# Weighting the attention logits and taking their maximum in one VectorE operation instead of two

## The reference, cut to what matters

```python
h = jnp.einsum('ni,hio->hno', x, W)                 # 4 heads, 64 features each
attn_src = jnp.einsum('hno,hod->hn', h, a_src)
attn_dst = jnp.einsum('hno,hod->hn', h, a_dst)
e = attn_src[:, src_idx] + attn_dst[:, dst_idx]     # one logit per edge and head
e = jnp.where(e >= 0, e, NEG_SLOPE * e)
e = e * edge_weight[None, :]
e_exp = jnp.exp(e - jnp.max(e))
denom = jax.ops.segment_sum(e_exp.T, dst_idx, num_segments=num_nodes).T
alpha = e_exp / (denom[:, dst_idx] + 1e-10)
msg = h[:, src_idx] * alpha[..., None]
out = jax.vmap(lambda m: jax.ops.segment_sum(m, dst_idx, num_segments=num_nodes))(msg)
```

## Time and profile before

| | |
|---|---|
| three runs | 818.95, 821.65, 824.38 us (median 821.65) |
| profiled execution | 820.17 us, span of the trace 818.0 us |
| busy: PE, DVE, POOL, ACT | 666.8, 593.3, 467.2, 224.4 us of the span |
| TensorE's granted clock, mean | 0.849 of full speed |

### The profile page before, as it was taken

How to read it: one execution, slowest core, us unless ns; L and a number is a source line. 1 busy time by engine, 2 the same in 40 slices (tenths; PEclk the granted TensorE clock), 3 DMA queues, 4 the chain that set the end, 5 groups by cost and what they waited for, 6 DMA issues and landing times.

```text
span 818.0 us, 18313 instructions
## 1 busy us (share of the span) xinstructions
PE 666.8 (82%) x4271; PEld 548.8 (67%) x4272; DVE 593.3 (73%) x1631; ACT 224.4 (27%) x817; POOL 467.2 (57%) x512
## 2 busy tenths in 40 slices
PE   3799687776878786878886878788859989999995
PEld 2577575554656564756675666666648879999994
DVE  7566268666767685867686868687789973989895
ACT  1132512111222122213232323232333423323331
POOL 5134246777777777777777777777721350333332
PEclk9899888887787678778677978686888989999998
DMA  7264325655556565656555555566410001000000
GB/s 212 58 181 75 87 72 114 138 138 136 134 135 143 131 139 134 140 133 138 137 135 134 139 135 138 132 138 140 108 35 1 1 12 71 33 26 27 27 27 22
DMA packets 104859, 82.97 MB, mean 101 GB/s; under 512 B 67133, under 2 KB 91566, under 8 KB 104561
## 3 DMA queue, kind: packets, MB, share of 16 engines
q0 software_dynamic: 18816, 52.21, 24.9%
q1 hardware_dynamic: 85873, 29.16, 16.8%
HBM read 74.47 MB, written 6.84 MB: 99 GB/s over the span
## 4 chain that ended last, share of the span: by engine, by line
PE 28%; issue 21%; DVE 17%; POOL 14%; DMA 11%; DVEq 5%; SPq 2%; ACT 1%; ACTq 0%; POOLq 0%
POOL G L380 13%; DMA G<-htab,srcr 9%; PE ps L552 8%; PE ps L565 8%; PE ps L414 4%; PE ps L474 4%; DVE msg L921 3%; PE ps L420 2%; DVEq L228 2%; DVE wprod L1079 1%; DMA x<-in_x 1%; DVE oh L983 1%; DVE G L1062 1%; DVE x L1066 1%; DVE x L1019 1%
## 5 line engine op out<-in xcount | busy, mean ns | idle before, releaser
L380 POOL DMA_INDIRECT G<-htab,srcr x392 | 372.9, 951 | 150.7 <-issue 127.7
L474 PE MATMUL ps<-msg,oh 128*128 128x260 f32 x784 | 265.9, 498 | 78.4 <-DVE oh L983 76.8
L474 PEld LDWEIGHTS ps<-msg,oh 128*128 128x128 f32 x784 | 183.0, 245 | 116.2 <-issue 83.3
L921 DVE TENSOR_TENSOR msg<-G,ps 128x1024 f32<-128x1024 f32 x98 | 118.7, 1212 | 29.1 <-issue 28.1
L552 PEld LDWEIGHTS ps<-xnT,w 128*128 128x128 f32 x800 | 98.3, 201 | 3.8 <-issue 1.8
L552 PE MATMUL ps<-xnT,w 128*128 128x128 f32 x800 | 98.8, 285 | 2.1 <-ACT wide L712 1.6
L656 ACT ACTIVATE msg<-et,negR 128x16 f32<-128x16 f32 x98 | 30.1, 308 | 224.2 <-DVE rj L915 178.7
L565 PE MATMUL ps<-w,wide 128*128 128x256 f32 x400 | 90.4, 380 | 1.0 <-DVE acc L1086 1.0
L565 PEld LDWEIGHTS ps<-w,wide 128*128 128x128 f32 x400 | 74.3, 190 | 10.2 <-issue 1.3
L393 POOL TENSOR_SCALAR G<-acc,mw 128x256 f32<-128x256 f32 x25 | 23.1, 923 | 99.6 <-DVE mw L1119 90.4
L983 DVE TENSOR_TENSOR oh<-ps,dmr 128x512 f32<-128x512 f32 x98 | 67.2, 686 | 17.0 <-issue 16.8
(11 more groups left out here) (135 smaller groups left out, 722.5 us busy)
## 6 DMA issues: line engine op xcount, KB each, us to landing
dstb<-dstu_d SPq DMA_DIRECT2D x98, 128.0 KB
G<-htab,srcr POOLq DMA_INDIRECT x392
htab<-hst SPq DMA_DIRECT2D x25, 130.0 KB, 2.8
out<-G SPq DMA_DIRECT2D x24, 128.0 KB, 1.7
x<-in_x SPq DMA_DIRECT2D x4, 640.0 KB, 8.0
w<-in_L_ffn_w SPq DMA_DIRECT2D x4, 512.0 KB
kq<-w_d SPq DMA_DIRECT2D x1, 1600.0 KB, 6.4
dmr<-dstm_d SPq DMA_DIRECT2D x98, 2.0 KB
```

The source lines that it names most:

```text
L380: gp.indirect_dma_start(G[:, q % RING, k, :], None, htab, bass.IndirectOffsetOnAxis(ap=srcr[:, q, k:k + 1], axis=0)).then_inc(s_g[q % RING ...
L474: m = pe.matmul(ps[:, 3 + p, 0:ROW], oh[:, p, k, :], msg[:, p, k, :], start=(k == 0), stop=(k == TILES - 1))
L921: dve.tensor_tensor(msg[:, p, :, 0:HF].rearrange("p k (h o) -> p k h o", h=HEADS), G[:, q % RING, :, 0:HF].rearrange("p k (h o) -> p k h o ...
```

## The change: one operation with an accumulator

`weight` and `reduce` become one operation: VectorE multiplies the logits by the edge weights, writes them, and keeps the largest product (starting from -3.0e38) in an accumulator, which goes into `rm`. It raises edge_max itself; the semaphore logit_weighted between the two is not used any more, and `reduce` does nothing. Between the wait for logit_leaky and the operation stands an increment of the semaphore dve_go, which nobody waits for.

```diff
                 def weight():
                     dve.wait_ge(S["logit_leaky"], ready)
-                    dve.tensor_tensor(e16, e16, wtr[:, q, :].unsqueeze(2).to_broadcast([P, TILES, HEADS]), ALU.mult).then_inc(S["logit_weighted"], 1)
+                    dve.sem_inc(S["dve_go"], 1)
+                    dve.tensor_tensor_reduce(e16, e16, wtr[:, q, :].unsqueeze(2).to_broadcast([P, TILES, HEADS]), 1.0, LOWEST, ALU.mult, ALU.max, rm[:, p:p + 1]).then_inc(S["edge_max"], 1)
 
                 def reduce():
-                    dve.wait_ge(S["logit_weighted"], ready)
-                    dve.tensor_reduce(rm[:, p:p + 1], e, AX.X, ALU.max).then_inc(S["edge_max"], 1)
+                    pass
                 return add, leak, weight, reduce
```

## The result

The changed kernel takes 826.64 us in the median of 22 runs, the kernel before 819.67 us in 22 runs beside them. The ratio is 1.0084, with a 95% interval of 1.0069 to 1.0099: 6.9 us, where 0.2 us was forecast and 3.1 us was the upper bound of the sum. The time lies outside the range of 818.8 to 825.0 us. The forecast of 821.9 us was put on three runs of the kernel before, whose median of 821.65 us is 2.0 us above that of the 22; so the time misses it by 4.7 us, and the change by 6.7. One run of the changed kernel took 1848 us; it is left out of the ratio and hardly moves the median.

The account below looks back on a forecast made before the run. GpSimd's pace of a gather every 1.25 us was taken to bound the loop. +0.1 us ahead of it, +0.0 in it and +0.1 behind sum to +0.2 us on 821.65 us: 821.9 us, range 818.8 to 825.0 us.

Parts of the forecast that it names:

- the upper bound of the sum: Whole kernel: +0.7 us ahead of the loop, +1.8 in it, +0.6 behind the last gather, +3.1 us in all.
- What bounds the loop: Edge loop, 126 to 598 us: GpSimd issues a gather every 1.25 us without interruption, 470 us for 376 gathers.
- The margin: Messages against GpSimd's gathers four groups later: 1.05 - 0.86 = 0.19 us at group 68, the tightest; typically 3.8 us.
- the sign that the prediction had named for being wrong: GpSimd in the loop: gaps opening behind L921 at groups 20, 36, 68 or 76 would refute the forecast.
- The price of the operation: VectorE, each group: 308 ns with its accumulator reading, against 339 ns removed; bounds 252 and 795 ns.
- The increment: VectorE's queue, each group: the new increment of dve_go costs 0.12 us, bounds 0 and 0.24 us.
- two instructions of the engine stay two: VectorE, each group: the 98 operations removed and added nearly cancel; with the increment, work changes by about +0.1 us.
- the upper bound of 0.70 us per group: VectorE's work per group at worst: 0.46 us for a dear operation plus 0.24 us for the increment.
- the loop, put at +0.0 us: Edge loop: GpSimd's pace hides all but group 68, +0.0 us; at most +1.2 there and +0.6 at group 20.
- the new operation holds up GpSimd: Rival at 97 logits: gathers wait for the whole operation, 0.31 us each, +30 us, time 852 us; chance 0.03.
- the new operation is dear: Rival in the loop: VectorE becomes late for GpSimd; trace bounds give +3 us, 825 us; chance of passing 1% 0.02.
- the earlier maximum shortens the loop: Rival in the loop: 71 groups gain some 0.2 us each from earlier edge_max, 14 us, time 808 us; chance 0.02.

Follow-up runs that it names:

- loop_only: The changed kernel, but with the two old operations in the copies ahead of the hardware loop, which so begins at its old place; ratio 0.9991.
- s18: The kernel before, with 18 idle increments at the start of VectorE's program, operations untouched; ratio 1.0011.
- s22: The kernel before, with 22 idle increments at the start of VectorE's program, operations untouched; ratio 1.0027.
- s26: The kernel before, with 26 idle increments at the start of VectorE's program, operations untouched; ratio 1.0047.
- q3off: The changed kernel, with the two old operations back in two of the eight groups of a pass; ratio 1.0080 to the kernel before.
- semonly: The kernel before with its two old operations, and only the increment of dve_go added between the wait and the multiplication; ratio 1.0081.
- again: The changed kernel measured once more, with nothing altered; ratio 1.0081 to the kernel before.
- a_256: The changed kernel, its loop moved by 256 instructions by a branch over 251 idle increments at the start; ratio 1.0051 to the kernel before.
- a_move: The changed kernel, its loop moved by 245 instructions by a branch over 240 idle increments at the start; ratio 1.0003 to the kernel before.

## Why the prediction was wrong, point by point

**What bounds the loop: right.** GpSimd's gathers at 1.25 us set it, and both the loss (gaps of GpSimd) and the gain of eight buffers came through them.

**The margin: right in size, and read too narrowly.** The 0.85 us between release and gather were as forecast, and gaps behind L921 opened, the sign that the prediction had named for being wrong. But of its groups 20, 36, 68 and 76 only 76 has one; the others are at 70, 77, 78 and 85, and group 68, the tightest of before with 1.05 us, has a slack of 1.85 us now. What was missing is why the slack dips once per pass. The idle 2.86 us ahead of L921 of group 64 stood in the very row that I used and was taken as given. Nothing was asked about what sets it.

**The price of the operation: right within its bounds.** 259 ns against 308 forecast and 252 as the lower bound; at 16 numbers the form costs no more than the plain product. **The increment: right**, 0.15 us against 0.12. Together the group costs VectorE +0.07 us in place of +0.1, and loop_only shows that this much, with the loop at its old place, changes nothing (0.9991).

**The step that failed** is the sentence that the operations removed and added cancel nearly, since "two instructions of the engine stay two", and with it the upper bound of 0.70 us per group. It priced what the engine and its queue do with each instruction. The third instruction in each copy also lengthens the program: it moves the hardware loop by 18 and makes it 16 longer. That puts an idle time of 1.3 us ahead of L983 into nine of ten passes, in place of 0.61 us behind it, which no price per group contains, since it depends on the place and not on the operation. So the loop, put at +0.0 us and at most +1.8, lost 4.9 us in the profiled execution. With the stalls alone (s18, s22, s26) the ratio is 1.0011 to 1.0047; with the first stall and the increments (q3off) 1.0080; with both stalls and all increments 1.0081 to 1.0084 (semonly, again, the changed kernel), but 1.0051 in a_256; with the increments alone 0.9991. So the loss does not look like a sum: the stall uses up the slack of the first groups of a pass, and the increments, hidden otherwise, then seem to be paid. For this speak the gaps in the traces, one execution each: over 0.30 us they lose 1.1 to 2.7 us with the stalls alone, and 3.9 to 5.0 us with the increments beside them. Against it stands the time of a_256, which is no longer than that of s26 without increments. The increments' part is therefore likely and not shown. The split between the fourth group's stall (s26 less s22, 0.2%) and the increments (q3off less s22, 0.5%) is not much sharper than their intervals, which are 0.15 to 0.2% to each side.

**The rivals.** That the new operation holds up GpSimd fell: the gathers' median is 947 ns, and semonly loses as much without it. That the new operation is dear fell with it. That the earlier maximum shortens the loop: TensorE's wait for it halved, and the time did not follow. The prediction also took 1% for the least that a measurement of this kernel tells from no change; the interval here is 0.15% to each side, and 0.84% is clear of it.

**The unchanged rest.** Behind the last gather 2.0 us more passed in this one profile. The same stretch takes 220.5 to 223.6 us in the kernels with four buffers, 222.1 in the second profile of the changed kernel and 220.9 in q3off, which loses as much. So it isn't shown that the change lengthens it.

**What stays open.** The three gaps ahead of the 114th, 218th and 322nd gather, 104 apart: at least one of them opens in every kernel with the stalls and four buffers, none in loop_only, a_move, the kernel before and the two with eight buffers. The trace names nothing that GpSimd waits for there. In the changed kernel they hold over half of what the gaps lose. And the new operation without the increment, with the wait on the operation itself, wasn't tried.

## What to carry to other kernels

Count the instructions that a change adds to an engine's program, ahead of a hardware loop and in it, and not only their time: the loop of 667 instructions here has stalls at branches whose place in the program decides, and a neutral edit can move one ahead of work that another engine waits for. Before believing a small loss or gain of an edit in such a loop, move the loop by idle instructions with the edit and without it. And where one engine's even pace sets a loop, look at the smallest margin of those who must not be late for it and at what makes it small; here eight buffers were worth 1.6%, or some 13 us, where the best that the prediction's sum allowed the fused operation was 0.2 us.

## What the runs showed of the hardware that was not expected

- A pass of VectorE's loop (667 instructions before, 683 with the change) begins with 3.1 to 3.3 us of idle time in the mean, in every kernel here, save the pass that is not entered by the jump back. Ahead of L983, behind a forward branch in its first group, 1.3 to 1.6 us more are idle in the mean where L983 has moved to place 230 or later, counted in steps of 256 instructions; at 219 or before the idle time falls ahead of the next addition of sums, with 0.6 to 1.2 us. The stall came back with a move by 256 (a_256) and left L983 with one by 245 (a_move).
- In the nine passes of the changed kernel that are entered by the jump back, VectorE goes on at L983 1.2 to 1.5 us behind the end of a packet on a DMA queue of the kind instruction; in the kernel before it goes on at L926, 1.3 to 1.6 us behind one.
- The product of 16 numbers with a maximum in the same operation takes 176 ns in the median and 178 in the mean, as long as the plain product (178 ns), and 83 ns for reading the accumulator; 256 numbers with a sum took 473 ns, 53 more than the plain product's 420. So the surcharge of the form is seen at 256 numbers and not at 16.
- A gather starts 0.85 us after the messages that it waited for, in each of the five waits for messages in the loop of the changed kernel, as in the one ahead of the loop.
